# Graph-layer kernel: dense product behind the fifth left-over block, candidate search at the step's end, results read one tile later, turned sums in a PSUM pair of their own

## The reference

```
def gcn_conv(x, edge_index, W, b, n_nodes):
    deg = segment_sum(ones, dst)                    # loops added
    dinv = where(deg > 0, rsqrt(deg), 0)
    h = x @ W.T
    out = segment_sum(h[src] * (dinv[src] * dinv[dst])[:, None], dst)
    return out + b

h = relu(gcn_conv(layernorm(x), edges, W1, b1))
x = x + gcn_conv(h, edges, W2, b2)                  # layer 2 adds the residual
x = x + soft_moe(layernorm(x))                      # needs row sums and the 32 slot logits of x
```

## Time and profile before

| | |
|---|---|
| time, median of 3 runs | 3240.34 us (3236.69 to 3242.41) |
| the profiled execution's own time | 3256.82 us |
| its span, first to last instruction | 3255.1 us |
| mean granted TensorE clock | 0.86 of full |
| busy: PE / DVE / POOL / ACT | 71% / 53% / 57% / 16% of the span |
| layer 1, from about 250 to 1600 us | 49 tiles |
| layer 2, from about 1660 to 3055 us | 49 tiles |

### The profile page before, as it was taken

The page is one execution under the profiler, slowest core; times in us unless marked ns, Lnnn a source line. Parts: engine busy times, 40 slices in busy tenths (PEclk is TensorE's granted clock), DMA queues, the critical chain, the costliest instruction groups (busy, mean ns, idle before and its releaser), DMA issues.

```text
span 3255.1 us, 27759 instructions
## 1 busy us (share of the span) xinstructions
PE 2324.9 (71%) x8202; PEld 1416.4 (44%) x8203; DVE 1715.2 (53%) x2250; ACT 531.2 (16%) x985; POOL 1847.1 (57%) x1857
## 2 busy tenths in 40 slices
PE   7536766777766676777666777777777777777798
PEld 7413444444444444444334444444444444444434
DVE  7654555555555555555445455554555555555516
ACT  7830000000000000000001111111111111111210
POOL 3356666666666666666366666666666666666100
PEclk9997888888888888888878888888888888888899
DMA  9597777778777777778488877887788787787747
GB/s 334 202 343 260 269 260 263 266 271 277 266 270 271 264 267 266 265 268 281 163 297 277 297 266 277 277 277 267 268 278 284 274 275 265 269 282 278 240 148 290
DMA packets 237826, 871.63 MB, mean 268 GB/s; under 512 B 64089, under 2 KB 64873, under 8 KB 237757
## 3 DMA queue, kind: packets, MB, share of 16 engines
q0 software_dynamic: 143808, 666.65, 60.4%
q1 hardware_dynamic: 66276, 162.56, 13.9%
q10 hardware_dynamic: 27692, 41.82, 3.5%
HBM read 826.10 MB, written 82.00 MB: 279 GB/s over the span
## 4 chain that ended last, share of the span: by engine, by line
issue 36%; another core or an unknown queue 30%; DVE 12%; PE 11%; ACT 2%; DMA 1%; DVEq 1%; POOL 0%; ACTq 0%; SPq 0%; POOLq 0%
DVE acc L1059 7%; PE work L1277 3%; PE left L1261 3%; PE left L1308 2%; DVE agg L1059 1%; ACT dump L660 1%; DVE before_end L970 1%; PE acc L1357 1%; PE fixed L1357 1%; PE left L1357 1%; DVE agg L1101 0%; PE work L1269 0%; PE acc L1333 0%; DMA xstage<-in_x 0%
## 5 line engine op out<-in xcount | busy, mean ns | idle before, releaser
L648 POOL DMA_INDIRECT rows<-table_layer,gidx x1764 | 1765.7, 1001 | 1010.5 <-issue 483.2
L1261 PE MATMUL left<-rows,hot 128*128 128x384 f32 x2352 | 981.3, 548 | 428.3 <-DVE agg L1101 327.3
L1277 PE MATMUL work<-WT,aggT 128*128 128x384 f32 x2352 | 915.0, 538 | 246.7 <-ACT aggT L763 225.1
L1059 DVE TENSOR_TENSOR acc<-acc,rows 128x768 f32<-128x768 f32 x1078 | 1037.2, 962 | 72.8 <-issue 28.4
L1261 PEld LDWEIGHTS left<-rows,hot 128*128 128x128 f32 x2352 | 480.6, 216 | 748.6 <-issue 532.2
L1277 PEld LDWEIGHTS work<-WT,aggT 128*128 128x128 f32 x2352 | 489.8, 211 | 626.5 <-ACT aggT L763 259.0
L977 DVE TENSOR_TENSOR pick_col<-slot_of,fixed 128x6 f32<-128x6 f32 x49 | 7.9, 161 | 571.3 <-remote 547.2
L1072 DVE SCALAR_TENSOR_TENSOR xs<-work,dinv,xs 128x768 f32<-128x768 f32 x49 | 49.9, 1017 | 481.6 <-PE work L1277 463.1
L771 ACT ACTIVATE ynext<-hid,dinv 128x768 f32<-128x768 f32 x49 | 45.8, 935 | 922.5 <-DVE hid L1067 905.5
L1269 PE MATMUL work<-ident,agg 128*128 128x128 f32 x588 | 118.3, 358 | 100.6 <-issue 73.7
L763 ACT ACTIVATE aggT<-work 128x768 f32<-128x768 f32 x98 | 79.4, 810 | 621.6 <-remote 428.8
(11 more groups left out here) (307 smaller groups left out, 1351.3 us busy)
## 6 DMA issues: line engine op xcount, KB each, us to landing
self_row<-table_layer SPq DMA_DIRECT2D x98, 384.0 KB
rows<-table_layer,gidx POOLq DMA_INDIRECT x1764
xstage<-in_x SPq DMA_DIRECT2D x67, 384.0 KB
xs<-in_x SPq DMA_DIRECT2D x58, 384.0 KB
table_layer<-ynext SPq DMA_DIRECT2D x49, 384.0 KB
xnew<-xs SPq DMA_DIRECT2D x49, 384.0 KB
table_layer<-xstage ACTq DMA_DIRECT2D x40, 384.0 KB
xstage<-xnew SPq DMA_DIRECT2D x21, 384.0 KB, 5.1
```

Of the source, the lines that this page charges most:

```text
L648: pool.indirect_dma_start(rows[:, slot, :], None, table[l][0:ROWS, :], bass.IndirectOffsetOnAxis(ap=gidx[:, k % 2, slot:slot + 1], axis=0) ...
L1059: dve.tensor_tensor(acc[:, :, 0:H] if n < OWN - 1 else halves(agg[:, :]), acc[:, :, 0:H], halves(row), ALU.add).then_inc(S["added"], 1)
L1261: m = pe.matmul(left[:, h, 0:H], hot[:, b, c, :], rows[:, slot, h * H:(h + 1) * H], start=c == 0, stop=c == LEFT - 1)
L1277: m = pe.matmul(work[:, h, 0:H], aggT[:, kc, :], WT[l][:, kc, h * H:(h + 1) * H], start=kc == 0, stop=kc == KC - 1)
```

## The change

It moves and renames; the arithmetic stays, except that layer 2's bias is added to the scaled product instead of to the residual.

- PE: all 12 matmuls of the dense product stand together behind block c = 4. In layer 1 they also wait for `left_ready` of the search for tile t+2, which lies in the two banks of `work` now. The search for tile t+3 stands at the end of PE's step. In layer 2 the turning of x (behind c = 2) and the logits (at the end) are those of tile t-3.
- DVE: the dense product is read one tile later, behind n = 7 of the next step (`scale_dense(2)`), the logits just before that. In layer 2 the bias is added in PSUM and the residual in an operation of its own.
- ACT and SP: the rows for the next layer, the measuring of rows, the store of the result and the load of residual rows are those of one tile earlier.
- PSUM: turned sums go to `fixed` (now also named `turned`), the small constants to the free ends of `acc`, the search's results to the free ends of `work`.

```diff
         fixed = ps("fixed", [P, 2, 512])
         tp, mm = work, left
-        bias2_ps, iota_ps = fixed[:, :, 0:H], fixed[:, 0, H:H + P]
-        found, pick_iota = fixed[:, 1, 0:LEFT * COLS].rearrange("p (c n) -> p c n", c=LEFT), fixed[:, 1, H:H + EXTRA]
+        turned = fixed
+        iota_ps, pick_iota = acc[:, 0, H:H + P], acc[:, 1, H:H + EXTRA]
+        found = work[:, :, H:H + LEFT // 2 * COLS].rearrange("p h (c n) -> p h c n", c=LEFT // 2)
...
+                    def store(back):
+                        side = (k - back) % 2
+                        out, src = (table[1], ynext) if l == 0 else (xnew, xs)
+                        sp.wait_ge(S["next_ready"], t - back + 1)
+                        sp.dma_start(out[ds((t - back) * P, P), :], src[:, side, :]).then_inc(S["stored"][side], 16)
...
-                    if not known or 1 <= t <= T:
-                        out, src = (table[1], ynext) if l == 0 else (xnew, xs)
-                        sp.wait_ge(S["next_ready"], t)
-                        sp.dma_start(out[ds((t - 1) * P, P), :], src[:, other, :]).then_inc(S["stored"][other], 16)
...
+                    elif not known or 2 <= t < T - 1:
+                        store(2)
+                        if l == 1 and (not known or t >= 3):
+                            load_res(1)
...
-                        if l == 0:
-                            act.wait_ge(S["scaled_ready"], t)
...
+                    if l == 0:
+                        if not known or 2 <= t < T:
+                            finish(2)
...
+                    else:
+                        if not known or 3 <= t < T:
+                            move_x(3)
+                        if not known or 2 <= t < T:
+                            stats(2)
...
                         else:
-                            xt = halves(xs[:, other, :])
-                            dve.wait_ge(S["res_biased"], t)
-                            dve.scalar_tensor_tensor(xt, work[:, :, 0:H], w, xt, ALU.mult, ALU.add
-                                                     ).then_inc(S["next_ready"], 1)
...
+                            xt = halves(xs[:, side, :])
+                            dve.scalar_tensor_tensor(work[:, :, 0:H], work[:, :, 0:H], w, halves(bias_bc[1][:, :]),
+                                                     ALU.mult, ALU.add).then_inc(S["res_biased"], 1)
+                            dve.wait_ge(S["res_in"][side], 16 * (i + (k - back) // 2 + 1))
+                            dve.wait_ge(S["res_biased"], t - back + 1)
+                            dve.tensor_tensor(xt, work[:, :, 0:H], xt, ALU.add).then_inc(S["next_ready"], 1)
...
                         if n >= 4 and n < 10 and l == 0 and (not known or t + 2 < T):
                             pick_left(t + 2, n - 4)
-                        if n == 8 and behind:
-                            if l == 1 and known and t == T:
+                            if n == 4 and (not known or t + 3 < T):
+                                mark_ends(t + 3)
+                        if n == 7 and (not known or 2 <= t < T - 1):
+                            if l == 1 and (not known or t >= 4):
+                                read_logits(4)
+                            scale_dense(2)
...
+                    def turn_agg(back, xs_moved):
+                        pe.wait_ge(S["agg_ready"], t - back + 1)
+                        if not known or t - back >= 1:
+                            pe.wait_ge(S["aggT_ready"], t - back)
+                        if l == 1 and (not known or xs_moved >= 1):
+                            pe.wait_ge(S["xT_ready"], xs_moved)
...
+                    def turn_x(back, aggs_moved):
+                        side = (k - back) % 2
+                        pe.wait_ge(S["next_ready"], t - back + 1)
+                        pe.wait_ge(S["aggT_ready"], aggs_moved)
...
+                    def dense(back, logits_read, parts=range(2 * KC)):
+                        if parts[0] == 0:
+                            pe.wait_ge(S["aggT_ready"], t - back + 1)
+                            if not known or t - back >= 1:
+                                pe.wait_ge(S["scaled_ready" if l == 0 else "next_ready"], t - back)
+                            if l == 1 and (not known or logits_read >= 1):
+                                pe.wait_ge(S["logit_read"], logits_read)
...
+                            if c == 0 and (not known or t >= 1):
+                                turn_agg(1, t - 3)
...
+                            elif c == 2 and l == 1 and (not known or t >= 3):
+                                turn_x(3, t)
+                            if c == 4 and not last:
+                                if l == 0 and (not known or t + 2 < T):
+                                    pe.wait_ge(S["left_ready"], t + 3)
+                                if not known or t >= 1:
+                                    dense(1, t - 3)
+                        if not last:
+                            if l == 0 and (not known or t + 3 < T):
+                                find_left(t + 3)
+                            if l == 1 and (not known or t >= 3):
+                                score(3)
```

More of the change, by code:

```diff
@@ L1043, in step @@
                     b, other = k % 2, (k + 1) % 2
[L1044 to L1045 removed]
+                    live = not known or t < T
                     def add_row(n):
@@ L1254, in step @@
+                    last = known and t == T - 1
+                    if not known or t < T:
+                        for c in range(LEFT):
                             slot = SLOT["left", c]
@@ L1272, in step @@
-                        if 1 <= c <= 3 and behind:
-                            if c == 1:
-                                pe.wait_ge(S["aggT_ready"], t)
-                            for part in range(4 * (c - 1), 4 * c):
-                                kc, h = divmod(part, 2)
-                                m = pe.matmul(work[:, h, 0:H], aggT[:, kc, :], WT[l][:, kc, h * H:(h + 1) * H],
-                                              start=kc == 0, stop=kc == KC - 1)
-                            if c == 3:
-                                m.then_inc(S["dense_done"], 1)
```

218 lines of the change are left out of this document (140 added, 78 removed).

## The result

The changed kernel takes 3067.16 us (median of 4 runs, 3058.95 to 3068.47) beside 3239.71 us for the kernel before: ratio 0.9462, interval 0.9443 to 0.9481. It is 5.4% faster, 172.6 us; 188 were forecast. The experiments add something that no row of this first pair could show: on other chips the same change makes the kernel 4.9% slower.

A forecast was written before the change was run, and what follows sets the result against it. No engine is full; a step is a cycle of waits, with PE's results seen late. 45 steps gain 1.4 us in layer 1 and 3.0 in layer 2, less 10 at the edges: 188 us, giving 3052 us, range 2890 to 3180.

The forecast's parts named there:

- the 16 us: Profiled execution of the kernel before over its 3240 us median; carried over, it turned the forecast 3069 us into 3052.
- Layer 1, 26.6 forecast: Layer 1's step falls from 28.0 to 26.6 us, set by row indices, product, block 5 and line 1101.
- the low clock: PE's clock stays low after idle time ahead of the product: 2.95 us lost in layer 1, 1.8 us in layer 2.
- the hold: Late in a long gather train, PE's results are held until POOL pauses and 1.4 to 2.2 us more.
- restart: POOL's next gather issue follows 0.87 us behind a released wait.
- Layer 2, 26.0 forecast: Layer 2's step falls from 29.0 to 26.0 us, set by POOL: 23.2 train, 1.9 hold, 0.87 restart.
- early turning: Layer 2's turning of `agg` no longer waits for the logits, ends at +2.3 us and is seen at once.
- rival B: Layer 2's early turning still held to +10.2 us; sign: ACT's copy starts over 5 us past 0; 3133 us; chance 0.18.
- C: Slower: POOL pauses twice a step, at its first batch for block 1 and for block 5; 29.2 us, 3313 us; chance 0.12.
- Rival D: The waits removed were not the path; both layers stay within 0.2 us of now, 3230 to 3250 us; chance 0.06.
- The edges: First and last steps' extra picks, product reads, turnings and logits: 10 us lost, bounds 0 and 25.
- Rival A: No PE result is held: layer 2 step 24.4 us, 2980 us, or 2881 with layer 1's clock kept high; chance 0.22.

The follow-up runs named there:

- e6: The kernel before, unedited, run again for its trace: 3222.55 us in its one run, beside 3239.79 us for its group.
- e10: The changed kernel, unedited, on a chip where the kernel before takes 2765.13 us: 2895.07 us, ratio 1.0485.
- e4: Changed kernel plus 16 unused matmuls filling PE's idle time ahead of layer 1's product, where the kernel before takes 2764.44 us: 2793.24 us.
- e11: Changed kernel with the dense product behind block 5 in both layers, on a chip where the kernel before takes 2765.13 us: 2764.37 us, ratio 0.9997.
- e12: Changed kernel with the dense product behind block 5 in both layers, on a chip where the kernel before takes 3226.18 us: 3066.39 us, ratio 0.9509.
- e5: The changed kernel, unedited, again, on a chip where the kernel before takes 3239.79 us: 3090.89 us, ratio 0.954.
- e8: Changed kernel gathering 256 of each row's 768 columns, on a chip where the kernel before takes 2765.08 us: 2897.92 us, ratio 1.0484.

## Why the prediction was right, and where it was not

**The sign and the size** hold for a holding chip. The profiled execution was forecast at 3069 us and took 3068.05. The median was forecast at 3052 and is 3067.16. The step that failed there is the last one: I took the 16 us by which the profiled execution of before stood over its median for a property of profiling. After the change the profiled execution stands 0.9 us over the median, and e6's, of the kernel before, stands 17 us under the median of its group. It was chance. So was part of the split: by e6's steps for before (28.6 and 28.0 us) the layers gain 2.1 and 1.6 us a step, together about 167 us, and not the 1.5 and 2.6 us of the result's pair. The gain of the medians is 172.6 us. That the forecast of 188 met the 188.8 us between the two spans is in part luck, since the profiled execution of before was a slow one.

**Layer 1, 26.6 forecast, 26.5 measured.** `row_idx` at +13.5 is exact, PE waits for it, DVE has no idle time at the first pick, and the step ends with block 5. Two terms cancel. The product took 10.26 us in the mean of 12 where 7.7 + 2.95 = 10.65 was forecast, so the low clock costs 2.3 us against the 8.0 of full clock; and DVE saw block 5 0.47 us behind the record's end, where 0.1 stood in the sum. That 0.47 is the hold at work here too: it is 2.02 us behind POOL's last issue (761.49), and train, hold and restart of this step (23.17, 2.02 and 0.76) also make 25.95 us. Over the 45 steps of 300 to 1500 us block 5 is seen 0.26 us late in the median and over 1.1 us in a tenth of them, against 0.11 in e10. Chain and hold end within some tenths of a us of each other, and no run on a holding chip tells which of them sets layer 1's 26.5. e4 measures the low-clock term by itself on a free chip, 10.41 - 8.01 = 2.4 us, and e10 and e11 show what the place of the product costs there, 2.6 us a step.

**Layer 2, 26.0 forecast, 26.4 measured.** In the result's trace the early turning was seen at once as taken (ACT at +4.4, under the 5 us of the sign), so rival B is out there. The product started at +11.8 as forecast. The term that was too small is the hold: 1.9 us behind POOL's pause was taken, 2.48 came, the step shown of e12 has 2.5 and that of e5 2.8 (2011.05 to 2013.87); the restart was 0.75 where 0.87 was taken. 0.4 us x 45 = 18 us. The low clock was taken ahead of the product, and the product ran at full clock in 7.98 us; nothing hung on it, since POOL was the bound, as said.

**Rivals B and C** named places of the hold that are real on another chip. In e5 the turning is held to +10.5 (B's sign) and POOL pauses at +7.7, at its first batch (C's place). After that pause block 5 is seen 0.6 us behind its record, and a second pause is mostly missing: 27.1 us in the mean of the 14 steps, not B's 27.8 or C's 29.2. Both priced the held result and then a further full wait behind it. In 8 of the 14 steps there is no second pause over 0.6 us, in 5 it is 0.6 to 1.3 us long, and in one (28.8 us) it is 2.7 us. So the forecast had the right pattern for the result's trace and for 27 of e5's steps, B and C had the right place in the other 14, and why e5 changes over at 2140 us isn't known. In the result's trace POOL pauses ahead of its third batch. **Rival D** is out by size. **The edges**: 45 x (1.5 + 2.6) = 185 us is nearly all of the 188.8 us between the two spans, so the 10 us lost at the edges didn't show in the profiled pair.

**Rival A, nothing is held,** is where the prediction was blind. Its mechanism is real, on three of five chips of the experiments, and its step of layer 2 (24.4, measured 23.4: no pause is left at all) and of layer 1 with a warm PE (24.4, e4 23.9) are near. The Trainium skill, Perfetto Trace Analysis, Tensor Engine Instruction, has the semaphore follow once PSUM has acknowledged the bytes; e10 and e11 agree with a signal that follows at once (0.1 and 0.04 us). The result and e12 have 4.4 and 7.9 us, and no row shows whether the acknowledgement or the signal is late there.

But A's sum was made against 3240 us. It treated the hold as something that the change might take away, while the hold belongs to the place where the kernel runs, and without it the kernel before is another kernel. It takes 2765 us there, and its 475 us less mean that it isn't bound by late results. That its steps are POOL's 23.5 us follows from its time, equal to e11's within 0.1%, not from a trace. The failing step is thus an unspoken one, that the profile's bound is the program's own. On a free chip there is nothing to win from the search's move, and the product in one piece ahead of block 5 costs: layer 1 goes from POOL's 23.5 to the chain's 26.1 us. e11, which moves only that product, takes back all of it (2895 to 2764 us).

On a holding chip the order hardly matters once there is one pause a step: e12 and the changed kernel have 26.5 and 26.4 to 26.5 us with the product on either side of block 5, since train, hold and restart make the step. The two stood on different chips, and two holding chips have 26.4 and 26.9 us for one and the same kernel. Of the parts of the change only the place of the product was varied on a holding chip; what the search's move and the early turning give there, each by itself, is read from the traces and wasn't run. So e12's version is the one to keep: within the intervals it is as fast as the changed kernel where results are held and as the kernel before where they aren't.

Two readings of the prediction are wrong and changed nothing. The turning that ends at 1957.87 is 4.4 us past its 0 (1953.45), not 3. And 703.14 to 725.43 is 1.311 us a gather, not 1.305, since one interval in it is 1.44 us long; in the result's layer 2 it is 1.302.

## What to carry to other kernels

An engine that stands idle behind a result which by its record is finished is a sign that the bound may lie with the chip at hand; take a second chip before tuning around it. Put long work that is read a step later behind the last block that gathers wait for, not ahead of it: here this cost nothing where results are late and was worth 2.6 us a step of layer 1 where they aren't. And an estimate made against the profiled execution shouldn't take over its distance to the median.

## What the runs showed of the hardware

The same kernel took 2764 to 2765 us in three groups of runs and 3226 to 3240 us in the others. Chip and occasion can't be told apart by these runs; the number of kernels in a group isn't the cause (two in both the second and the fourth).

Of PE, DVE and ACT only PE signals late. A trace holds, beside the instructions, the events of the semaphores, by which one engine tells another that a result is there. Of the 650 events of PE that the result's trace has between 250 and 2880 us, 239 come over 0.5 us behind the end of the record that they belong to, 191 of them while POOL pauses. Of the 1308 events of DVE and ACT none does. In e10 none of 1038 of PE's does; there the event stands 0.01 us behind the record. So "until POOL pauses" is the rule of most late results and not of all: 48 of the 239 came through while POOL issued on.

On holding chips the profile also lacks what it has on free ones, the time to landing of most transfers. The DMA issues of e12:

```profile
self_row<-table_layer SPq DMA_DIRECT2D x98, 384.0 KB
rows<-table_layer,gidx POOLq DMA_INDIRECT x1764
```

and of e11:

```profile
self_row<-table_layer SPq DMA_DIRECT2D x98, 384.0 KB, 6.7
rows<-table_layer,gidx POOLq DMA_INDIRECT x1764, 5.5
```

The page of before has no landing time in these rows either. The transfers' signals aren't held like PE's. In the step of e12 above DVE adds the row of the gather issued at 2135.67 at 2141.78, 6.1 us later and in the middle of the train that holds PE's results. What is missing is their events in the record: the traces have 15175 to 21289 semaphore events on holding chips and 37299 to 41956 on free ones.

That leaves a rival which no run tests, the recording itself. Each run on record has a span and a clock of its own, so it seems that each was recorded, and the chips that lose events are those that hold results. Whether a kernel that isn't recorded takes 3067 or 2895 us there isn't known. Whether POOL's issuing or the transfers' traffic brings the hold about is open as well: the one run that would tell, e8, met a free chip.

A gather of 128 rows is issued each 1.30 us whether its rows have 3 KB or 1 KB (308 issues in 400 us in e10 and in e8); in the page of e8 it lands in 2.8 us:

```profile
rows<-table_layer,gidx POOLq DMA_INDIRECT x1764, 2.8
```
